# Transformer layer with perturbed experts: the key change split in four parts, the second expert's weights perturbed during the first expert's last batch, the signals' credits given by five engines

## The chip, the cores and the metric

One NeuronCore of a Trainium2 chip runs the whole program. The metric is the device time in microseconds (us), the median of several executions. The engines are TensorE (PE; PEld is its weight load), VectorE (DVE), ScalarE (ACT), GpSimd (POOL) and SyncE (SP), which issues most of the transfers.

## What is computed

Eight batches of 512 tokens with 256 features pass through a cross-attention over 64 context rows (16 heads) and a layer of 8 experts. Expert 0 has the clean weights and experts 1 to 7 all have the same perturbed weights, so the layer needs two experts, with weights p0 and the sum of the other seven probabilities.

```python
def _perturb_attractive(w, scale=0.8, sparsity=0.1):
    a = jnp.abs(w)
    k = max(1, int(n * sparsity / 2))
    s = jnp.sort(flat)
    thr_bot, thr_top = s[k - 1], s[n - k]
    tier = jnp.where(a >= thr_top, -1.0, jnp.where(a <= thr_bot, 1.0, 0.0))
    return w + scale * w * tier
...
x = x + attention(layernorm(x), ctx)           # 16 heads, softmax over 64 keys
h = layernorm(x_in) * gamma + beta             # router
probs = softmax(h @ Wr + br)
pre = x_in @ W1s[e] + b1s[e];  y = gelu(pre) @ W2s[e] + b2s[e]
out = sum_e probs[e] * y[e]
```

## The kernel before, in words

**Order.** Every engine runs a hand-written program; semaphores join them. A prologue loads weights and runs the attention of batch 0. `pipeline` then runs `body(i)` for i = 1 to 7: the attention of batch i beside the first (clean) expert on batch i - 1. `last_expert` runs the clean expert on batch 7, and a loop runs the second (perturbed) expert on batches 0 to 7, with x and the accumulator read back from DRAM.

**Products.** Each fp32 product is made of three matmuls of a high and a low part (`three`, lines 355 to 357). In an expert a batch has eight hidden products (`hidden`, 128x512 into `ps_l`) and eight output products (`output`, into `ps_y`). ACT makes the gelu and its high part in `region_c_hi` (lines 996 and 999), and the low part in `region_c_lo` is made by POOL in the first expert (`low_part`, line 1237) and by DVE in the second (line 1800). `output` waits for the low part, and `hidden` for the high part of two steps before.

**The search.** The eight thresholds (top and bottom of W1, W2, b1, b2) are found by bisection on the bits of |w|: 15 steps on the upper halfword, then 16 on the lower (`BITS`). A step is compares on DVE (`compare`, line 1455) and ACT (line 968), counts on PE (line 732), a total (line 738) and `decide` on DVE. Four steps stand in each body. Between the two rounds, in body 3 (`TURN`), DVE builds new keys from the lower halfwords: `second_round` (lines 1507 to 1536), four tensor_scalar and four tensor_tensor on 128x2048 uint16, then small instructions, the start of the new state, and only then `normalise_output(i, 0)`, for which the attention's value product `values(i, 1)` on PE waits.

**Perturbation.** In `last_expert` DVE makes the perturbed weights (`perturb`, lines 1747 to 1760: five instructions on 128x2048 fp32 for each of W1 and W2, the same on 128x8 and 128x256 for the biases), splits them into high and low parts over the clean weights (`split`, lines 1312 and 1314), splits x of batch 0 and mixes batch 7 of the first expert (`mix`, line 1440). PE's first hidden product of the second expert waits for the low part of x.

**Start.** The semaphores are counted up without a reset, so each signal first gets one batch of credit: a block of its own, in which POOL increments all 85 signals one by one (lines 368 to 372), with a barrier of all engines behind it.

## Time and profile before

| | us |
|---|---|
| median of 3 runs | 751.48 (751.09 to 755.43) |
| the profiled execution | 758.23 |
| its span, first to last instruction | 756.4 |
| PE busy in it | 672.9 (89%) |
| DVE busy in it | 517.6 (68%) |
| ACT, POOL busy | 381.6, 272.6 |

The span is what the traces show; 1.8 us of the profiled execution's own time lie around it. The profile reads in rows: the start, the time busy, the engine, the line of the program, what is written and from what, and in brackets how long the engine sat idle before it and what released it. PE's clock in a stretch is given as a share of full speed: 1.00 is 2.4 GHz, 0.5 is 1.2 GHz.

### The profile page before, as it was taken

The numbers are of one execution on the slowest core, as the hardware profiler recorded it, in microseconds if no ns is written. First come the engines' busy times: TensorE is split into PE (matmuls) and PEld (weight loads), VectorE is DVE, ScalarE is ACT, GpSimd is POOL, SyncE is SP. The second block draws the span as 40 slices with busy tenths as digits, with TensorE's granted clock in tenths as the row PEclk, the third lists the DMA queues.
The fourth block names the chain that finished last, engine by engine and source line by source line (L and its number), as shares of the span: only waits on it lengthen the run. The fifth ranks groups of instructions, "written<-read, shape, count | busy, mean of one in ns | idle before, by whom it ended". The sixth has DMA issues, their size and how long they took to land.

```text
span 756.4 us, 15501 instructions
## 1 busy us (share of the span) xinstructions
PE 672.9 (89%) x5555; PEld 613.3 (81%) x5555; DVE 517.6 (68%) x1205; ACT 381.6 (50%) x490; POOL 272.6 (36%) x284
## 2 busy tenths in 40 slices
PE   1758869999999399999999999999929999999996
PEld 1647858899889399889889899888828888898886
DVE  2778786786798869889888777653993445443452
ACT  2445226746747255855855855645304444445442
POOL 2343461673573358367366346325700000000000
PEclk9876577998999699999999998799959999999998
DMA  4996302622722440560640550231102221122221
GB/s 148 205 197 143 55 31 83 116 51 86 136 53 79 86 84 29 142 108 30 153 93 28 129 92 29 85 112 72 41 0 84 84 83 38 58 71 83 83 56 28
DMA packets 131797, 63.62 MB, mean 84 GB/s; under 512 B 104603, under 2 KB 122021, under 8 KB 131749
## 3 DMA queue, kind: packets, MB, share of 16 engines
q1 hardware_dynamic: 121652, 60.43, 32.9%
q10 hardware_dynamic: 10096, 2.56, 1.8%
q8 instruction: 29, 0.48, 0.3%
q14 instruction: 20, 0.16, 0.1%
HBM read 35.69 MB, written 23.09 MB: 78 GB/s over the span
## 4 chain that ended last, share of the span: by engine, by line
PE 67%; DVE 18%; issue 5%; SPq 4%; DMA 2%; ACT 2%; ACTq 0%; POOL 0%; DVEq 0%; POOLq 0%
PE ps_m L654 7%; PE ps_l L355 7%; PE ps_y L355 7%; PE ps_y L356 7%; PE ps_y L357 7%; PE ps_l L357 6%; PE ps_l L356 6%; PE ps_m L732 4%; DVE ind L1455 4%; PE ps_s L622 4%; PE ps_s L642 3%; DVE region_b L1430 3%; PE ps_m L694 2%; PE ps_s L355 2%; PE ps_s L357 1%
## 5 line engine op out<-in xcount | busy, mean ns | idle before, releaser
L996 ACT ACTIVATE region_b<-ps_l,bias 128x512 f32<-128x512 f32 x128 | 88.0, 687 | 172.5 <-PE ps_l L357 170.5
L355 PE MATMUL ps_y<-w_hi,region_c_hi 128*128 128x256 f32 x512 | 149.0, 291 | 0.0
L356 PE MATMUL ps_y<-w_lo,region_c_hi 128*128 128x256 f32 x512 | 146.7, 286 | 0.0
L357 PE MATMUL ps_y<-w_hi,region_c_lo 128*128 128x256 f32 x512 | 145.9, 285 | 0.0
L355 PE MATMUL ps_l<-x2s_hi,w_hi 128*128 128x512 f32 x256 | 108.8, 425 | 15.4 <-DVE x2s_lo L1314 14.8
L1237 POOL TENSOR_TENSOR region_c_lo<-region_b,region_c_hi 128x512 fp32r<-128x512 f32 x64 | 94.5, 1482 | 66.6 <-ACT region_c_hi L999 66.6
L1800 DVE TENSOR_TENSOR region_c_lo<-region_b,region_c_hi 128x512 fp32r<-128x512 f32 x64 | 44.3, 693 | 96.5 <-ACT region_c_hi L999 96.5
L357 PE MATMUL ps_l<-x2s_hi,w_lo 128*128 128x512 f32 x256 | 103.1, 403 | 0.0
L356 PE MATMUL ps_l<-x2s_lo,w_hi 128*128 128x512 f32 x256 | 102.9, 402 | 0.0
L356 PEld LDWEIGHTS ps_y<-w_lo,region_c_hi 128*128 128x128 f32 x512 | 98.6, 193 | 2.1
L355 PEld LDWEIGHTS ps_y<-w_hi,region_c_hi 128*128 128x128 f32 x512 | 98.5, 192 | 2.0
L999 ACT ACTIVATE region_c_hi<-ps_l,bias 128x512 fp32r<-128x512 f32 x128 | 87.5, 683 | 25.2 <-PE ps_y L357 25.2
L357 PEld LDWEIGHTS ps_y<-w_hi,region_c_lo 128*128 128x128 f32 x512 | 98.6, 193 | 0.0
L1455 DVE TENSOR_SCALAR ind<-key,cand 128x2048 bf16<-128x2048 uint16 x93 | 97.7, 1089 | 0.0
L1211 POOL TENSOR_TENSOR region_a<-region_a,mx 128x1024 f32<-128x1024 f32 x32 | 62.0, 1940 | 97.5 <-DVE mx L1356 97.5
L968 ACT ACTIVATE ind<-key,cand 128x2048 bf16<-128x2048 uint16 x31 | 62.0, 1999 | 48.3 <-DVE cand L1485 46.1
L654 PE MATMUL ps_m<-vbd,region_a 128*128 128x34 f32 x512 | 69.5, 295 | 15.6 <-DVE on L1366 15.4
L654 PEld LDWEIGHTS ps_m<-vbd,region_a 128*128 128x128 f32 x512 | 67.9, 214 | 16.4 <-issue 16.2
L355 PEld LDWEIGHTS ps_l<-x2s_hi,w_hi 128*128 128x128 f32 x256 | 49.6, 194 | 28.6 <-issue 16.4
L732 PEld LDWEIGHTS ps_m<-ones_bf,ind 128*128 128x128 bf16 x1488 | 45.3, 98 | 20.8 <-issue 16.6
L732 PE MATMUL ps_m<-ones_bf,ind 128*128 128x1 bf16 x1488 | 50.0, 164 | 11.3 <-DVE ind L1455 10.4
L357 PEld LDWEIGHTS ps_l<-x2s_hi,w_lo 128*128 128x128 f32 x256 | 49.5, 193 | 11.7
(200 smaller groups left out, 1228.1 us busy)
## 6 DMA issues: line engine op xcount, KB each, us to landing
qs<-q_scr SPq DMA_DIRECT2D x16, 512.0 KB, 6.5
acc_scr<-acc SPq DMA_DIRECT2D x8, 514.0 KB, 5.0
acc<-acc_scr SPq DMA_DIRECT2D x8, 514.0 KB, 3.4
xa<-in_x SPq DMA_DIRECT2D x8, 512.0 KB, 5.6
q_scr<-qn_lo SPq DMA_DIRECT2D x16, 256.0 KB, 5.0
x<-in_x SPq DMA_DIRECT2D x32, 128.0 KB, 3.9
xt_scr<-region_b SPq DMA_DIRECT2D x8, 512.0 KB, 2.6
region_b<-x SPq DMA_DIRECT2D x8, 512.0 KB, 3.1
```

The lines of the kernel that those rows point to most:

```text
L355: eng.matmul(out_ap, a[0], b[0], start=first, stop=False)
L356: eng.matmul(out_ap, a[0], b[1], start=False, stop=False)
L357: return eng.matmul(out_ap, a[1], b[0], start=False, stop=last)
L654: mm = pe.matmul(ps_m[:, 0, n * VW:(n + 1) * VW], pT[:, j % 2, n * P:(n + 1) * P], vbd[:, n, :], start=True, stop=True)
L732: mm = pe.matmul(ps_m[:, 1, s:s + 1], ind[s][:, c * P:(c + 1) * P], ones_bf[:, 0:1], start=c == 0, stop=c == WN // P - 1)
L968: act.activation(ind[3][:], key[:, key_of[rnd][3], :], ACT.Sign, bias=cand[:, 3:4], scale=-1.0, accum_out=signs[:]).then_inc(signs_summed. ...
L996: act.activation(g[:, f % 4, :], ps_l[:, f % 2, :], ACT.Gelu_apprx_tanh, bias=bias[:, e, f:f + 1]).then_inc(s["gelu"].handle, 1)
L999: act.activation(gs[0][:, f % 4, :], ps_l[:, f % 2, :], ACT.Gelu_apprx_tanh, bias=bias[:, e, f:f + 1]).then_inc(s["g_hi"].handle, 1)
L1211: pool.tensor_tensor(m, m, mx[:, j, :].unsqueeze(2).to_broadcast([P, H, CT]), ALU.subtract).then_inc(s_shifted.handle, 1)
L1237: pool.tensor_tensor(gs[1][:, f % 4, :], g[:, f % 4, :], gs[0][:, f % 4, :].bitcast(F32), ALU.subtract).then_inc(s["g_lo"].handle, 1)
L1455: dve.tensor_scalar(ind[s][:], key[:, key_of[rnd][s], :], cand[:, s:s + 1], None, ALU.is_le).then_inc(ind_ready.handle, 1)
L1800: dve.tensor_tensor(gs[1][:, f % 4, :], g[:, f % 4, :], gs[0][:, f % 4, :].bitcast(F32), ALU.subtract).then_inc(s["g_lo"].handle, 1)
```

## The change

**Credits.** Five engines give every fifth credit each, in the same block before the same barrier.

**Key change.** `second_round` becomes four parts in DVE's body 3: `end_first_round` (the prefix), then the normalisations of value tiles 0 and 1 with the queries' low parts between them, `lower_keys(0)` (half of the large instructions), more of the body, `lower_keys(1)` behind the normalisation of tile 3, and `start_second_round` (small instructions) behind the projection's low part (`low_output`).

**Perturbation.** W1 and W2 are loaded again into the search's four mark tiles `ind` (as fp32, each weight in two halves), once the last total is known, not into `region_a`. DVE perturbs W1's first half behind the statistics of batch 7 in body 7, its second half before `mix` of batch 6, and W2, the biases and the low parts between the eight low parts of the gelu of the first expert on batch 7, which move from POOL to DVE. ACT makes the high parts of the perturbed weights (four activations of 128x1024) and the normalised x of batch 7 that POOL made. The perturbed split weights go into tiles that are free by then (`qs`, `kbd`, `xhT`, `qn`), so that the clean ones stay.

**Order of the second expert.** It begins with batch 7, whose x, x's split and accumulator are still in place, and goes on with batches 0 to 6.

```diff
     with nc.Block() as credit:
+        def give(eng, share):
+            for s in signals[share::5]:
+                eng.sem_inc(s.handle, s.per)
...
         @credit.gpsimd
         def _(pool):
-            for s in signals:
-                pool.sem_inc(s.handle, s.per)
+            give(pool, 4)
...
-                wait(sp, o_product, i)
-                sp.dma_start(wagain[:, 0].rearrange("p (c f) -> p c f", c=DC), W1.rearrange("(c p) f -> p c f", p=P)).then_inc(ld_again[0], 16)
-                sp.dma_start(wagain[:, 1].rearrange("p (c d) -> p c d", c=FC), W2.rearrange("(c p) d -> p c d", p=P)).then_inc(ld_again[1], 16)
...
+                wait(sp, total_ready, sum(BITS) - 1)
+                for h in range(2):
+                    sp.dma_start(wagain[0][h], W1[h * P:(h + 1) * P, :]).then_inc(ld_again[0], 16)
+                for h in range(2):
+                    sp.dma_start(wagain[1][h].rearrange("p (c d) -> p c d", d=D),
+                                 W2.rearrange("(c p) d -> p c d", p=P)[:, h * FC // 2:(h + 1) * FC // 2]).then_inc(ld_again[1], 16)
...
             more_gelu(5)
+            if last:
+                wait(act, ln[1]["shift"], i)
+                for t in range(NT):
+                    act.activation(xh[1][:, t, :], x2[:, t, :], ACT.Identity, bias=shiftby[1][:, t:t + 1],
+                                   scale=rstd[1][:, t:t + 1]).then_inc(ln[1]["xhat"].handle, 1)
...
                 gelu(0, B - 1, f)
+                if f == 1:
+                    act.wait_ge(pw_ready, 2)
+                    for h in range(2):
+                        act.activation(w1p[0][:, h * F:(h + 1) * F], wagain[0][h], ACT.Copy).then_inc(pw_hi, 1)
+                if f == 6:
+                    act.wait_ge(pw_ready, 4)
+                    for h in range(2):
+                        act.activation(w2p[0][h], wagain[1][h], ACT.Copy).then_inc(pw_hi, 1)
...
+        def low_gelu(e, b, f):
+            s = ex[e]
+            wait(dve, s["g_hi"], b, f + 1)
+            wait(dve, s["y_step"], b if f >= 4 else b - 1, f - 3 if f >= 4 else f + 5)
+            dve.tensor_tensor(gs[1][:, f % 4, :], g[:, f % 4, :], gs[0][:, f % 4, :].bitcast(F32), ALU.subtract).then_inc(s["g_lo"].handle, 1)
...
             if turn:
-                second_round()
+                end_first_round()
...
             cmp(0, 2)
+            if turn:
+                lower_keys(0)
             probabilities(i - 1)
+            if turn:
+                normalise_output(i, 2)
...
             normalise_output(i, 3)
+            if turn:
+                lower_keys(1)
             base(0, i - 1)
             dec(0)
             low_output(i)
+            if turn:
+                start_second_round()
             cmp(1, 0, 1, 2)
             add_residual(i)
             stats(1, i, x2)
+            if last:
+                thresholds()
+                mark_weights(0, 0)
+                perturb_weights(0, 0)
...
             low_x2(i)
+            if last:
+                mark_weights(0, 1)
+                perturb_weights(0, 1)
...
         def last_expert():
...
+            low_gelu(0, B - 1, 0)
+            mark_weights(1, 0)
+            low_gelu(0, B - 1, 1)
+            perturb_weights(1, 0)
+            low_gelu(0, B - 1, 2)
+            low_weights(0)
+            low_gelu(0, B - 1, 3)
+            mark_weights(1, 1)
+            low_gelu(0, B - 1, 4)
+            perturb_weights(1, 1)
+            low_gelu(0, B - 1, 5)
+            dve.wait_ge(pw_ready, 4)
+            perturb_hidden_bias()
+            low_gelu(0, B - 1, 6)
+            perturb_output_bias()
+            low_gelu(0, B - 1, 7)
+            low_weights(1)
             probabilities(B - 1)
             base(0, B - 1)
```

DVE in body 3, from the end of the first round. `ind<-key,prefix` and `key<-ind,key` are the key change, `rs` and `on` a tile's normalisation (for PE's next value product), `qn_lo` the queries' low part. Before:

```order
L1505 COPY prefix<-cand 128x8
L1519 TENSOR_SCALAR ind<-key,prefix 128x2048 x2
L1523 TENSOR_TENSOR key<-ind,key 128x2048
L1524 TENSOR_TENSOR key<-ind,key 128x2048
...
L1501 MEMSET half 128x1
L1361 RECIPROCAL rs<-ps_m 128x16
L1366 TENSOR_TENSOR on<-ps_m,rs 128x8x16 x2
L1336 SCALAR_TENSOR_TENSOR qn_lo<-ps_s,bq,qn_hi 128x512 x2
```

And with the change:

```order
L1553 COPY prefix<-cand 128x8
L1411 RECIPROCAL rs<-ps_m 128x16
L1416 TENSOR_TENSOR on<-ps_m,rs 128x8x16 x2
L1386 SCALAR_TENSOR_TENSOR qn_lo<-ps_s,bq,qn_hi 128x512 x2
L1411 RECIPROCAL rs<-ps_m 128x16
L1416 TENSOR_TENSOR on<-ps_m,rs 128x8x16 x2
L1568 TENSOR_SCALAR ind<-key,prefix 128x2048 x2
L1571 TENSOR_TENSOR key<-ind,key 128x2048
L1572 TENSOR_TENSOR key<-ind,key 128x2048
```

Two normalisations and the queries' low part now stand ahead of the first half of the key change.

DVE further on in body 3, around the projection. `region_d_lo` is the low part for which PE's projection waits, `region_b<-b2row` the first expert's base, `x<-ps_s,x` the residual. Before:

```order
L1366 TENSOR_TENSOR on<-ps_m,rs 128x8x16 x2
L1430 SCALAR_TENSOR_TENSOR region_b<-b2row,p,region_b 128x256 x4
L1374 TENSOR_TENSOR region_d_lo<-ps_s,region_d_hi 128x1024
L1455 TENSOR_SCALAR ind<-key,cand 128x2048 x3
L1459 TENSOR_TENSOR sind<-skey,cand 128x32
L1381 TENSOR_TENSOR x<-ps_s,x 128x512 x2
```

And with the change:

```order
L1416 TENSOR_TENSOR on<-ps_m,rs 128x8x16 x2
L1568 TENSOR_SCALAR ind<-key,prefix 128x2048 x2
L1571 TENSOR_TENSOR key<-ind,key 128x2048
L1572 TENSOR_TENSOR key<-ind,key 128x2048
L1478 SCALAR_TENSOR_TENSOR region_b<-b2row,p,region_b 128x256 x4
L1424 TENSOR_TENSOR region_d_lo<-ps_s,region_d_hi 128x1024
L1578 TENSOR_SCALAR smark<-skey,prefix 128x8
L1580 TENSOR_TENSOR skey<-smark,bias 128x8
```

The second half now stands between the last tile's normalisation and the low part for the projection, and the small instructions between that and the compares.

DVE from the mix of batch 6 (`acc<-ps_y,p,region_b`) on. Before:

```order
L1440 SCALAR_TENSOR_TENSOR acc<-ps_y,p,region_b 128x256 x4
L1505 COPY prefix<-cand 128x8
L1766 CAST thr<-prefix 128x8
L1756 TENSOR_SCALAR key<-region_a 128x2048
L1757 TENSOR_SCALAR region_a<-key,thr 128x2048
L1758 SCALAR_TENSOR_TENSOR region_a<-key,thr,region_a 128x2048
L1759 TENSOR_SCALAR region_a<-region_a 128x2048
L1760 SCALAR_TENSOR_TENSOR region_a<-region_a 128x2048
```

And with the change:

```order
L1488 SCALAR_TENSOR_TENSOR acc<-ps_y,p,region_b 128x256 x4
L1759 TENSOR_TENSOR region_c_lo<-region_b,region_c_hi 128x512
L1729 TENSOR_SCALAR key<-ind 128x1024
L1730 TENSOR_SCALAR key<-key,thr 128x1024
L1731 SCALAR_TENSOR_TENSOR key<-key,thr 128x1024
L1759 TENSOR_TENSOR region_c_lo<-region_b,region_c_hi 128x512
L1735 TENSOR_SCALAR key<-key 128x1024
L1736 SCALAR_TENSOR_TENSOR ind<-key,ind 128x1024
L1759 TENSOR_TENSOR region_c_lo<-region_b,region_c_hi 128x512
L1765 TENSOR_TENSOR kbd<-ind,qs 128x1024 x2
```

The gelu's low parts (`region_c_lo`) stand on DVE now, between pieces of the perturbation of half a weight.

## Rows read from the trace of the kernel before

**Rows 1.** Page, part 4: the chain that ended last, shares of the span by engine.

```profile
PE 67%; DVE 18%; issue 5%; SPq 4%; DMA 2%; ACT 2%; ACTq 0%; POOL 0%; DVEq 0%; POOLq 0%
```

**Rows 2.** PE's waits: line, releaser: us in total, times, longest.

```profile
PE ps_m L654 <- DVE on L1366: 15.4, 2, 11.8
PE ps_l L355 <- DVE x2s_lo L1314: 14.8, 1, 14.8
```

**Rows 3.** The credit block's instructions (line 368): duration ns, start us.

```profile
L368 DVEq DRAIN  x1: 10/10/10, 0.8 to 0.8; - x1
L368 POOLq DRAIN  x1: 41/41/41, 7.8 to 7.8; - x1
L368 PEldq EVENT_SEMAPHORE  x1: 51/51/51, 8.0 to 8.0; - x1
```

**Rows 4.** DVE in order of time in body 3: start, us, what, [idle before].

```profile
245.81 1.42 DVE L1519 TENSOR_SCALAR ind<-key,prefix 128x2048 uint16<-128x2048 uint16 x2
...
249.66 1.89 DVE L1519 TENSOR_SCALAR ind<-key,prefix 128x2048 uint16<-128x2048 uint16 x2
255.33 1.22 DVE L1527 TENSOR_SCALAR smark<-skey,prefix 128x8 uint16<-128x8 uint16 x1
258.35 0.26 DVE L1361 RECIPROCAL rs<-ps_m 128x16 f32<-128x16 f32 x1
262.90 0.26 DVE L1361 RECIPROCAL rs<-ps_m 128x16 f32<-128x16 f32 x1 [2.46 <-PE ps_m L654]
270.00 0.26 DVE L1361 RECIPROCAL rs<-ps_m 128x16 f32<-128x16 f32 x1 [3.64 <-PE ps_m L654]
273.18 0.26 DVE L1361 RECIPROCAL rs<-ps_m 128x16 f32<-128x16 f32 x1 [2.40 <-PE ps_m L654]
277.00 1.21 DVE L1374 TENSOR_TENSOR region_d_lo<-ps_s,region_d_hi 128x1024 fp32r<-128x1024 f32 x1
281.50 1.28 DVE L1381 TENSOR_TENSOR x<-ps_s,x 128x512 f32<-128x512 f32 x2
```

**Rows 5.** Windows: PE, PEld, DVE, ACT, POOL busy, granted clock, DMA share, GB/s.

```profile
248.00:259.00 11.00, 0.00 (x0) 0.00 (x0) 10.56 (x24) 2.56 (x3) 6.72 (x4) 0.61 0.35 56
259.00:268.00 9.00, 8.73 (x38) 8.07 (x39) 4.72 (x22) 1.02 (x1) 0.00 (x0) 0.53 0.48 86
```

**Rows 6.** POOL in order of time in body 3: a low part beside the key change.

```profile
250.96 1.71 POOL L1237 TENSOR_TENSOR region_c_lo<-region_b,region_c_hi 128x512 fp32r<-128x512 f32 x1
```

**Rows 7.** DVE in order of time, from body 7's low part of x on.

```profile
520.91 1.22 DVE L1341 TENSOR_TENSOR x2s_lo<-region_b,x2s_hi 128x1024 fp32r<-128x1024 f32 x1
544.66 0.16 DVE L1756 TENSOR_SCALAR sabs<-bias 128x8 uint32<-128x8 uint32 x1
545.80 1.23 DVE L1756 TENSOR_SCALAR key<-region_a 128x2048 uint32<-128x2048 uint32 x1
554.35 0.29 DVE L1756 TENSOR_SCALAR key<-b2row 128x256 uint32<-128x256 uint32 x1
556.38 1.23 DVE L1312 CAST w_hi<-region_a 128x2048 fp32r<-128x2048 f32 x1
559.85 0.69 DVE L1312 CAST x2s_hi<-region_b 128x1024 fp32r<-128x1024 f32 x1
565.18 1.65 DVE L1440 SCALAR_TENSOR_TENSOR acc<-ps_y,p,region_b 128x256 f32<-128x256 f32 x4
566.75 0.68 DVE L1800 TENSOR_TENSOR region_c_lo<-region_b,region_c_hi 128x512 fp32r<-128x512 f32 x1
```

**Rows 8.** PE in order of time: the second expert's first matmul.

```profile
562.14 0.76 PE L355 MATMUL ps_l<-x2s_hi,w_hi 128*128 128x512 f32 x1 [14.82 <-DVE x2s_lo L1314]
```

**Rows 9.** Windows, columns as in rows 5, of the last batch of expert 0 and beyond.

```profile
523.90:547.40 23.50, 23.42 (x149) 20.77 (x147) 22.39 (x27) 10.13 (x16) 16.93 (x8) 1.00 0.20 68
562.00:568.00 6.00, 5.86 (x14) 4.63 (x15) 5.40 (x7) 1.55 (x3) 0.00 (x0) 0.51 0.06 23
585.40:608.50 23.10, 23.02 (x145) 20.41 (x145) 10.55 (x19) 10.13 (x16) 0.00 (x0) 1.00 0.24 69
```

More of the change, by code:

```diff
@@ L175, in build_program @@
     ind = [sb(f"ind{n}", [P, WN], BF16) for n in range(4)]
+    wagain = [[ind[2 * n + h][:].bitcast(F32) for h in range(2)] for n in range(2)]
+    mag, tier = (key[:, 2 * n:2 * n + 2].rearrange("p a n -> p (a n)").bitcast(F32) for n in range(2))
     sind = sb("sind", [P, 4, FC])
@@ L1288, in body @@
             rsqrt(1, i)
-            normalise(1, i, x2, 0, 1, 2, 3)
+            if not last:
+                normalise(1, i, x2, 0, 1, 2, 3)
             low(5)
@@ L1301, in last_expert @@
         def last_expert():
[L1302 to L1303 removed]
+            pass
         pipeline(pool, body, last_expert)
@@ new lines, in low_weights, with thresholds @@
+        def low_weights(n):
+            for h in range(2):
+                hi, lo = ([w[:, h * F:(h + 1) * F] for w in w1p], [w[h] for w in w2p])[n]
+                dve.wait_ge(pw_hi, 2 * n + h + 1)
+                i = dve.tensor_tensor(lo, wagain[n][h], hi.bitcast(F32), ALU.subtract)
+            i.then_inc(pw_lo, 1)
+        def thresholds():
+            wait(dve, cand_step, sum(BITS) - 1)
+            take_prefix()
+            dve.wait_ge(state_ready, NS + 13)
+            dve.tensor_copy(thr[:, :, 0], prefix[:]).then_inc(thr_ready, 1)
+            dve.wait_ge(thr_ready, 2)
```

191 lines of the change are left out of this document (100 added, 91 removed).

## The prediction

> **What bounds the kernel now.** The chain of work that ended last comes first: PE holds 67% of the span's time on it, DVE 18% [rows 1]. With 672.9 of 756.4 us busy, PE is the bound almost everywhere, so a change pays only where PE stands still or runs at its lower clock. Where that is, PE's list of waits shows: 15.4 us for a normalised value tile from DVE (one wait is 11.8) and 14.8 us for the low part of x in front of the second expert [rows 2]. The windows then show what such a hole costs beyond itself: after the first, PE's granted clock is 0.53 for 9 us, that is the 1.2 GHz level for nearly all of it [rows 5], and after the second it is 0.51 for 6 us [rows 9]. In full batches without a hole it is 1.00, and a batch of an expert takes 23.1 to 23.5 us [rows 9]. The third idle place is the start: POOL comes to the end of the credit block at 7.8 us and DVE at 0.8 us, and everything waits for the barrier at 8.0 [rows 3]. The change touches these three places.
>
> **The credits.** POOL spends 7.8 - 0.8 = 7.0 us on 85 increments, 82 ns each [rows 3]. Of the 85 each engine now gives 17: 17 x 82 ns = 1.4 us. PE may be slower: one semaphore instruction of its sequencer takes 51 ns where POOL's own are near 17 in the same view; with 51 - 17 = 34 ns more each, PE needs 17 x 116 ns = 2.0 us. The barrier waits for the slowest, so the gain is 5.0 to 5.6 us; I take 5.3. What follows it depends on nothing earlier and moves as a whole. No row shows two engines incrementing at once; if increments go one at a time, whoever gives them, the gain is 0. That is the lower bound, 5.6 the upper.
>
> **The key change.** From its first instruction to the residual, DVE needs 281.50 - 245.81 = 35.7 us. In that time it idles 2.46 + 3.64 + 2.40 = 8.5 us, each time for a value product of PE [rows 4], and PE makes these late since it stood still for 11.8 us and then ran at 1.2 GHz. So DVE waits for a PE that has waited for DVE. The change takes the normalisation of tile 0 from 258.35 to about 245.8: behind the prefix, whose product is ready. PE goes on at once at full clock. The work of DVE is the same: 35.7 - 8.5 = 27.2 us. To it I add what is left of idle time, about 1 us (for the high part of the queries and for value product 1, both a few tenths late), and contention: the first half of the large instructions took 249.66 - 245.81 = 3.85 us with POOL mostly idle, the second 255.33 - 249.66 = 5.7 us while POOL made low parts [rows 4, 6]. Both halves now lie beside POOL's work, which adds 5.7 - 3.85 = 1.8 us. That makes 30.0 us and a gain of 5.7 at the residual.
>
> PE gets a new hole. Its program from value product 1 to the projection is three value products, two transposes, three hidden products, one more transpose and two output products, some 15 us; with its small waits it stands before the projection at about 263. There it needs the low part `region_d_lo`, which DVE makes behind `lower_keys(1)`: 259.4 + 5.7 + 3.1 for the base (273.88 to 277.00 in rows 4, whose third wait ends at 273.18 with 0.7 of normalisation behind it) + 1.2 = 269.4. So PE idles some 6 us there and its clock may fall as in [rows 5]; the projection would take 5 us and not 3. This is mostly covered: the next thing for which PE waits, the residual, comes from DVE at 245.8 + 30.0 = 275.8, later than PE needs it. I take the gain as 6.0: 5.7, and 0.3 of the small instructions of which one took 1.22 us beside POOL at 255.33 and its fellows 0.2. Bounds: 3 (more contention, clock low to the end of the stage) and 8.5 (all idle time gone, no more contention).
>
> At this place a rule speaks against the change. The rows show that contention lengthened four large instructions by 1.8 us in all [rows 4, 6]. The Trainium skill (SBUF, "Who interferes with whom") says that DVE in a two-port mode, or with two SBUF inputs against a reading GpSimd, and GpSimd exclude each other for whole instructions. By that rule each of the four instructions could wait out one POOL low part.
>
> **The perturbation.** Now DVE needs from the mix of batch 6 until 562 for what PE waits for. The new chain of DVE starts at the low part of x, 520.91 + 1.22 = 522.1 [rows 7]. Prices: one whole weight takes 554.35 - 545.80 = 8.55 us in five instructions. A whole cast takes 1.23 and a half one 0.69 [rows 7], so the fixed part of an instruction is 2 x 0.69 - 1.23 = 0.15 us; half a weight is (8.55 + 5 x 0.15) / 2 = 4.65, say 4.8 with the semaphores between. The whole cast and subtraction take 559.85 - 556.38 = 3.47 us, so a subtraction in two halves, with the cast gone to ACT, is 2.4. Output bias: 556.38 - 554.35 = 2.0. Hidden bias: 545.80 - 544.66 = 1.1. A low part of the gelu: 0.63 in a row (0.68 by itself). Mix: 1.6. POOL has nothing left to do there, so no contention is added.
>
> W1's first half, 4.8 us, goes into DVE's idle time behind the statistics of batch 7 (it waits for the router until 520) and costs nothing; without that cover it would cost 4.8. W1's second half ends at 522.1 + 4.8 = 526.9, mix at 528.5. Then 8 low parts 5.0, two halves of W2 9.6, W1's low part 2.4, biases 1.1 + 2.0: 20.1 us, until 548.6. The last output product (12 matmuls, 1.4 us) waits for this: PE ends the first expert at 550.1 instead of 547.3. That is 2.8 us late, since between these points PE has 23.4 us of work from 523.9 [rows 9] and DVE has 26.5 from 522.1: DVE is the bound there by a little, with the PE's waits spread over the last three output products. ACT's four new activations (1.03 each by a 128x1024 activation elsewhere in the trace) delay gelu 2 and 7 by some 2 us each, while PE has output products in hand.
>
> PE then starts the second expert at 550.2 in place of 562.14 [rows 8]: 11.9 us. Its x is in place, its W1 is ready since about 537. Behind it DVE still has W2's low part 2.4, probabilities and base 2.5, mix 1.6, until 555.2; PE's first output product of the second expert waits for that mix but comes after four hidden products, 550.2 + 5.9 = 556.1. And the clock stays: before, 14 matmuls took 5.86 us at the lower level, which at 2.4 GHz would be half, 2.9 us; since PE then waits for the gelus a little, I count 2.4. Sum 14.3. Bounds: 11 (clock fell anyway or each half a fifth dearer) and 16 (no lateness of DVE).
>
> The moves of xhat to ACT, of the reload to the four `ind` tiles and of batch 7 to the front of the second expert cost nothing: four activations against four POOL instructions of the same length; W1 has from the last total near 497 until 511, where before 2 MB had from 499 until 526; and the loads of the other batches run a batch ahead as before. If W1 came late, DVE's idle time until 520 covers 4 us of it.
>
> **Sum.** 5.3 + 6.0 + 14.3 = 25.6 us. Against the profiled execution 758.23 - 25.6 = 732.6. The median of the runs is 6.75 us lower than that execution, and I take the same difference from it: 751.48 - 25.6 = 725.9, or 3.4% less.
>
> **The rivals.**
> (a) The credits bring nothing, because increments are taken one at a time. For it: no row shows them side by side. Against it: each engine's instructions in the block are its own. 751.48 - 20.3 = 731.2.
> (b) The hole in body 3 only moves to the projection. By the exclusive turns each of four DVE instructions waits for a POOL low part of 1.71 us [rows 6]: 4 x 1.71 = 6.8 us where I count 1.8 in the second half, so 5 us of my 6 are lost, and PE runs the projection and the next products at 1.2 GHz. Against it: the measured second half, beside two POOL low parts and two bias additions, was only 1.8 longer. 751.48 - 20.6 = 730.9. This is the outcome of the rule of the SBUF page named above.
> (c) The last batch of the first expert becomes bound by DVE more than counted, its instructions a fifth dearer: 26.5 x 0.2 = 5.3 us. PE's stall is spread in pieces at each output product. 731.2.
> (d) Slower than before: the waits for DVE spread through that last batch lower PE's clock and it does not come back in the second expert's loop. A batch of 23.1 us takes then 46. The gain of 25.6 is eaten after 25.6 / 23.1 = 1.1 batches at 1.2 GHz; with two such batches the time would be 751.48 - 25.6 + 46.2 = 772. For it: PE at 1.2 GHz after each hole. Against it: it came back within 6 to 9 us of steady work each time [rows 5, 9].
>
> **How the numbers follow.** My forecast, all three places within 4 us of the sum: 0.70. (a) 0.06, (b) 0.10, (c) 0.09, (d) 0.02, and 0.03 for a gain of under 7.5 us from something not seen. The range takes the three middle rivals in and goes down to all upper bounds but 1 us each: 725.9 - 5 = 721, up to 733, two of them half come true. A measurement of this kernel can tell about 1%, 7.5 us, from no change. (a), (b) and (c) are all faster by over 1%; so faster 0.95, same 0.03, slower 0.02.
>
> **What would show it.** DVE's first instruction near 2.5 us in place of 8.2. PE's wait of 11.8 us for DVE's `on` gone, and in its place one of 4 to 7 us for `region_d_lo` in body 3; DVE's half changes at 3.9 to 5.7 us each. The wait of 14.8 us gone, waits of 1 to 3 us in all for `region_c_lo` in the last batch, the first expert's end some 3 us later after the last low part of x, the second expert's first four hidden products at clock 1.00. I would be wrong if DVE's instructions beside POOL took much over 2 us, if PE's clock were under 0.9 over the last 200 us, or if W1's reload ended DVE's wait.

## The result, and the profile after

The changed kernel takes 727.1 us (median of 4 runs, 724.2 to 731.6) beside 753.1 (751.1 to 755.4) for the kernel before: a ratio of 0.966, 95% interval 0.960 to 0.972. Measured again later beside other kernels it took 725.1 us (6 runs), ratio 0.964 (0.958 to 0.970). Forecast were 725.9 us, range 721 to 733. In some executions of a kernel the mean clock is lower and the time over 1.5% longer; ratios and intervals leave these out, medians do not.

The whole program first. This is the page of the kernel after: its span, the busy times, PE's granted clock in 40 slices (tenths of full speed), and the chain that ended last.

```profile
span 724.9 us, 15487 instructions
PE 664.5 (92%) x5555; PEld 605.1 (83%) x5555; DVE 512.1 (71%) x1221; ACT 386.9 (53%) x498; POOL 257.5 (36%) x271
PEclk9776577999999979999999999989999999999999
PE 65%; DVE 19%; issue 5%; SPq 4%; DMA 3%; ACT 1%; ACTq 0%; DVEq 0%; POOL 0%; POOLq 0%
```

The chain hardly differs from [rows 1]: PE 65% where it had 67. PE has the same 5555 matmuls and is busy 8.4 us less, mostly since more of them ran at the full clock. The span is 31.5 us shorter. The profiled execution of before took 758.2 us, 5.1 above its median, so the two traces differ by 5.5 us more than the medians, which differ by 26.0.

The three places, in order of time. First the start: the increments (line 374) by engine, with duration in ns and the first and last start, then the transfer of x that follows the barrier, of after and of before (ACT, not shown, lies between SP and POOL).

```profile
L374 SPq EVENT_SEMAPHORE  x18: 17/17/17, 0.7 to 1.7; - x18
L374 POOLq EVENT_SEMAPHORE  x17: 17/17/17, 0.7 to 1.9; - x17
L374 DVEq EVENT_SEMAPHORE  x17: 21/21/21, 0.8 to 2.2; - x17
L374 PEldq EVENT_SEMAPHORE  x17: 51/51/51, 0.8 to 3.3; - x17
```
```profile
3.66 0.45 SPq L425 DMA_DIRECT2D xa<-in_x  x1
```
```profile
8.09 0.46 SPq L403 DMA_DIRECT2D xa<-in_x  x1
```

Four engines are done by 2.2 us, PE at 3.3: (3.3 - 0.8) / 16 = 0.16 us from one to the next, against 0.06 to 0.09 on the others. The barrier that ended behind 7.8 us in [rows 3] now ends at 3.6. The transfer was issued at 8.09 before: 4.4 us gained.

Next DVE in body 3, which answers [rows 4]. The large instructions of `lower_keys` are lines 1568 to 1572; line 1478 is the base, line 1424 the low part for the projection, line 1431 the residual. First the prefix before, which [rows 4] leave out:

```profile
245.60 0.17 DVE L1505 COPY prefix<-cand 128x8 f32<-128x8 f32 x1
```

And after:

```profile
240.19 0.17 DVE L1553 COPY prefix<-cand 128x8 f32<-128x8 f32 x1
240.39 0.26 DVE L1411 RECIPROCAL rs<-ps_m 128x16 f32<-128x16 f32 x1
...
244.50 2.66 DVE L1568 TENSOR_SCALAR ind<-key,prefix 128x2048 uint16<-128x2048 uint16 x2
247.20 1.63 DVE L1571 TENSOR_TENSOR key<-ind,key 128x2048 uint16<-128x2048 uint16 x1
248.75 2.30 DVE L1572 TENSOR_TENSOR key<-ind,key 128x2048 uint16<-128x2048 uint16 x1
...
256.83 0.26 DVE L1411 RECIPROCAL rs<-ps_m 128x16 f32<-128x16 f32 x1 [1.78 <-PE ps_m L683]
...
257.52 1.89 DVE L1568 TENSOR_SCALAR ind<-key,prefix 128x2048 uint16<-128x2048 uint16 x2
...
262.14 2.82 DVE L1478 SCALAR_TENSOR_TENSOR region_b<-b2row,p,region_b 128x256 f32<-128x256 f32 x4
264.88 1.21 DVE L1424 TENSOR_TENSOR region_d_lo<-ps_s,region_d_hi 128x1024 fp32r<-128x1024 f32 x1
...
270.12 1.46 DVE L1431 TENSOR_TENSOR x<-ps_s,x 128x512 f32<-128x512 f32 x2
```

The first value tile is normalised right behind the prefix. From the prefix to the residual DVE takes 270.12 - 240.19 = 29.9 us. Before it was 35.9, from the copy of the prefix at 245.60 to 281.50 in [rows 4]: 6.0 gained. PE's side, a line of its list of waits and two of its rows in order of time; the third row is that of value product 3 in a second profile of the same changed kernel:

```profile
PE ps_m L683 <- DVE on L1416: 6.4, 2, 3.7
```
```profile
253.19 3.60 PE L683 MATMUL ps_m<-vbd,region_a 128*128 128x34 f32 x16 [2.73 <-DVE on L1416]
...
266.24 0.38 PE L357 MATMUL ps_s<-wqp_hi,region_d_hi 128*128 128x256 f32 x1 [2.90 <-DVE region_d_lo L1424]
```
```profile
249.65 1.95 PE L683 MATMUL ps_m<-vbd,region_a 128*128 128x34 f32 x16 [2.73 <-DVE on L1416]
```

The wait of 11.8 us in [rows 2] is gone. In its place body 3 has 2.73 us for value tile 2, which stands behind `lower_keys(0)`, and 2.90 us in front of the projection. Behind the first of these waits PE ran at the lower clock level, 1.2 GHz: value product 3 takes 3.60 us, from 253 to 257 us the clock is 0.50, and from 253.19 to 263.35 us the granted clock is 0.68. In the second profile the wait is the same 2.73 us, but the clock is 1.00 until 251.00, falls only about 2 us after the product's start (0.57 from 251.50 to 255.50), and the product takes 1.95. The wait of 3.7 lies at 72 us, in batch 0; before, it was the other of the two in [rows 2].

Last, the second expert: PE's first matmul of it, the low part of x ahead of it on DVE, and PE's waits for the gelu's low parts.

```profile
507.01 1.22 DVE L1391 TENSOR_TENSOR x2s_lo<-region_b,x2s_hi 128x1024 fp32r<-128x1024 f32 x1
...
535.47 0.39 PE L357 MATMUL ps_l<-x2s_hi,qs 128*128 128x512 f32 x1
```
```profile
PE ps_y L357 <- DVE region_c_lo L1759: 1.4, 2, 0.8
```

From DVE's low part of x to the second expert it is 535.47 - 507.01 = 28.5 us; before, 562.14 - 520.91 = 41.2 [rows 7, 8]: 12.8 gained. The wait of 14.8 us is now two waits of together 1.4 us inside the last batch of the first expert. From there to the end of the span it is 724.9 - 535.47 = 189.4 against 756.4 - 562.14 = 194.3: 4.8 more. The windows say where the first part of that lies (PE, PEld, DVE, ACT, POOL busy, granted clock, DMA share, GB/s). Of before, the first 8 us of the second expert, then of after some of the same work:

```profile
562.00:566.00 4.00, 3.85 (x9) 3.11 (x10) 3.97 (x5) 0.84 (x2) 0.00 (x0) 0.50 0.01 2
566.00:570.00 4.00, 4.00 (x14) 2.94 (x14) 2.12 (x5) 2.42 (x5) 0.00 (x0) 0.77 0.33 132
```
```profile
542.00:546.00 4.00, 4.00 (x29) 3.66 (x29) 1.32 (x3) 2.17 (x4) 0.00 (x0) 1.00 0.00 0
```

A clock of 0.50 and 0.77 over 4 us each is 2.0 + 0.9 = 2.9 us of PE's time at full clock. After, the clock is 1.00. The other 1.9 us are shorter batches, which were no part of the change's plan. The times at which the accumulator's load is issued give a batch's length, of before (first two lines, five batches apart) and of after:

```profile
594.72 0.35 SPq L564 DMA_DIRECT2D acc<-acc_scr  x1
...
710.44 0.35 SPq L564 DMA_DIRECT2D acc<-acc_scr  x1
```
```profile
587.77 0.35 SPq L592 DMA_DIRECT2D acc<-acc_scr  x1
...
702.34 0.35 SPq L592 DMA_DIRECT2D acc<-acc_scr  x1
```

That is 115.72 / 5 = 23.14 us and 114.57 / 5 = 22.91, so 8 batches give 1.8.

The account of the two traces: start 4.4, body 3 6.0, to the second expert 12.8, behind it 4.8, together 28.0 of 31.5. The other 3.5 lie between these places: 1.0 between the first transfer and the prefix, where the code is the same, and 2.5 between the residual and x of the last batch, where it is the same but for body 7. The last section shows that stretches with the same code differ by such amounts from one execution to the next.

### The profile page after: what moved, and what is told of

Same layout as the page of the kernel before. It is cut to its first block, busy times and chain, and to the rows that moved or that the text cites. A ratio compares the mean times of both kernels' runs of the same rounds, so it can differ in the third digit from the quotient of the medians.

```text
span 724.9 us, 15487 instructions
## 1 busy us (share of the span) xinstructions
PE 664.5 (92%) x5555; PEld 605.1 (83%) x5555; DVE 512.1 (71%) x1221; ACT 386.9 (53%) x498; POOL 257.5 (36%) x271
## 4 chain that ended last, share of the span: by engine, by line
PE 65%; DVE 19%; issue 5%; SPq 4%; DMA 3%; ACT 1%; ACTq 0%; DVEq 0%; POOL 0%; POOLq 0%
PE ps_l L357 8%; PE ps_m L683 7%; PE ps_l L359 7%; PE ps_l L358 7%; PE ps_y L357 5%; PE ps_y L358 5%; PE ps_y L359 5%; PE ps_m L769 4%; PE ps_s L651 4%; PE ps_s L671 3%; DVE ind L1503 3%; DVE region_b L1478 2%; PE ps_s L357 2%; PE ps_m L723 2%; PE ps_s L359 2%
## 5 line engine op out<-in xcount | busy, mean ns | idle before, releaser
L357 PE MATMUL ps_y<-w_hi,region_c_hi 128*128 128x256 f32 x256 | 76.3, 298 | 1.4 <-DVE region_c_lo L1759 1.4
L359 PE MATMUL ps_y<-w_hi,region_c_lo 128*128 128x256 f32 x256 | 73.3, 286 | 0.0
L358 PE MATMUL ps_y<-w_lo,region_c_hi 128*128 128x256 f32 x256 | 73.3, 286 | 0.0
L769 PEld LDWEIGHTS ps_m<-ones_bf,ind 128*128 128x128 bf16 x1488 | 45.2, 98 | 19.9 <-issue 17.6
L357 PE MATMUL ps_l<-x2s_hi,w_hi 128*128 128x512 f32 x128 | 55.6, 434 | 0.1
L357 PE MATMUL ps_l<-x2s_hi,qs 128*128 128x512 f32 x128 | 52.0, 407 | 2.2 <-DVE x2s_lo L1364 1.9
L359 PE MATMUL ps_l<-x2s_hi,w_lo 128*128 128x512 f32 x128 | 51.7, 404 | 0.0
L358 PE MATMUL ps_l<-x2s_lo,w_hi 128*128 128x512 f32 x128 | 51.6, 403 | 0.0
L651 PE MATMUL ps_s<-kbd,qs 128*128 128x256 f32 x256 | 49.2, 327 | 2.2 <-DVE region_a L1400 1.2
L359 PE MATMUL ps_l<-x2s_hi,kbd 128*128 128x512 f32 x128 | 50.4, 394 | 0.0
L358 PE MATMUL ps_l<-x2s_lo,qs 128*128 128x512 f32 x128 | 50.4, 394 | 0.0
```

The source lines that it names most:

```text
L357: eng.matmul(out_ap, a[0], b[0], start=first, stop=False)
L358: eng.matmul(out_ap, a[0], b[1], start=False, stop=False)
L359: return eng.matmul(out_ap, a[1], b[0], start=False, stop=last)
L651: mm = pe.matmul(ps_s[:, m, (g % 2) * D:(g % 2) * D + D], qs[:, g, j * P:(j + 1) * P], kbd[:, n, g].rearrange("p h k -> p (h k)"), start=n ...
L769: mm = pe.matmul(ps_m[:, 1, s:s + 1], ind[s][:, c * P:(c + 1) * P], ones_bf[:, 0:1], start=c == 0, stop=c == WN // P - 1)
```

## The experiments

**Each part alone.** Three kernels each have one of the three parts on top of the kernel before. The edits are the three pieces of the diff shown above.

> The kernel before with only the credits given by five engines. Theory (the three parts of the change add up, and the start moves as a whole): the first transfer starts at 3.7 us as in the changed kernel, where it started at 8.09 [rows 3 show the barrier at 8.0], and the time falls by 4.4 us, not the 5.3 of the forecast, since PE is the last to finish its share. Rival 1 (increments are taken one at a time): first transfer at 8 us, gain 0. Rival 2 (the earlier start runs into a transfer that lands at the same time as before): first transfer at 3.7, but the first projection of body 1 at 150.9 as before, gain under 1 us.

Measured: 748.8 us against 753.8, ratio 0.994 (0.991 to 0.997), so 4.6 us (2.1 to 7.1). The transfer of x is issued at 3.66 us, as in the changed kernel, and the first projection of body 1 starts at 146.18 us, where it was 150.95: the whole gain arrives there. The increments of several engines do run side by side.

> The kernel before with only the key change split in four. Theory: body 3's residual comes 6.0 us after where it did, counted from the prefix instruction (30.0 in place of 35.9 us from prefix to residual), and the time falls by 6 us. Rival 1 (the hole moves to the projection and its cost with it): a wait of PE of 5 us or more for the low part in front of body 3's projection, PE's clock under 0.7 for the 9 us behind it, gain 3 or less. Rival 2 (what is gained in body 3 is given back in bodies 4 and 5, where DVE is late): the same 30.0 us in body 3, but under 4 us in the whole.

Measured: 746.6 us, ratio 0.990 (0.985 to 0.994), so 7.9 us, with an interval of 4.2 to 11.5. The execution that was profiled took 757.9 us, 11 more than the median, so only its order and its local waits are read: from the prefix at 244.67 to the residual at 273.19 it is 28.5 us, 7.4 less than before, and PE's wait in front of the projection 2.6. The hole does not just move.

> The changed kernel with the credits and the key change as before, so that only the perturbation, the weights' reload, and the order of the second expert's batches are changed. Theory (the term of the forecast, 14.3, and the sum of parts): gain 14.3 to 16.5 us, the upper value if the second expert's batches are each 0.25 us shorter as in the changed kernel (22.92 against 23.17 between starts of batches). Rival 1 (the clock at the second expert's start is worth nothing by itself): 12. Rival 2 (the shorter batches come from the earlier key change or credits): batches of 23.17 us here.

Measured: 736.2 us, ratio 0.976 (0.972 to 0.981), so 17.9 us (14.6 to 21.3). From the low part of x at 516.51 to the second expert's first matmul at 544.97 it is 28.5 us, as in the changed kernel, and a batch takes 22.92. Body 3 is that of before (a wait of 11.7 us for the normalised tile).

The gain is above the 14.3 to 16.5 expected. The three ratios multiplied give 0.960, the whole change 0.966 and 0.964, each with about 0.006 to either side. Within these intervals the parts add up; that one gives back 3 or 4 us of another they don't exclude, but no trace shows it. What the new order of the batches, the reload and ACT's copies bring or cost each was not measured apart.

**The credits without PE.** In the changed kernel:

```diff
-            for s in signals[share::5]:
+            for s in signals[share::4]:
...
-        @credit.tensor
-        def _(pe):
-            give(pe, 1)
```

> The changed kernel with the credits given by four engines, all but PE. In the changed kernel PE's 17 increments took from 0.8 to 3.3 us, those of SP, ACT and POOL until 1.9 at the latest, DVE's until 2.2. Theory (the barrier waits for PE, whose increments take 0.15 us each, others 0.06 to 0.08): with 21 or 22 each, DVE ends near 2.6 and the first transfer starts at 2.9 to 3.1 us in place of 3.66; gain against the changed kernel 0.6 to 0.8 us. Rival (increments slow each other, and fewer givers do not help): first transfer at 3.6 or later.

Measured: 722.9 us, ratio 0.960 (0.956 to 0.965). The slowest engine, DVE, gives its last increment at 2.6 us, and x is asked for 0.70 us earlier, by SP's row of that transfer:

```profile
2.96 0.45 SPq L421 DMA_DIRECT2D xa<-in_x  x1
```

The difference of 4.3 us to the first measurement of the changed kernel was more than the start can bring, so both were run again side by side.

> The changed kernel as it is, again, beside the next one, so that the two are measured on the same chip in the same rounds. Theory (PE's increments of 0.15 us each end the credit block 0.7 us later than four engines would): this kernel 0.5 to 1.5 us slower than the next one. Rival (the earlier difference of 4.3 us between separate calls was real, since PE's increments cost something beyond the start): 3 to 5 us slower. 725 to 728 expected.

> The changed kernel with the credits given by SP, ACT, POOL and DVE alone, again. Theory: 0.5 to 1.5 us faster than the changed kernel, the later start being all. Rival: 3 to 5 us faster, about 722 to 723, as it was measured in another call.

Measured: 725.1 and 723.9 us (0.964 and 0.960; both intervals reach 0.005 to 0.006 to either side). The difference is 1.2 us, and the first transfer again stands at 3.66 and 2.96. What the trace shows of it is 0.7 us. The 4.3 us between separate calls were for the most part scatter. Leaving PE out is right by the trace; whether it makes the whole faster is within the intervals.

**Is DVE or the hole the bound in body 3?** The second half of the keys is put behind the projection's low part, so that PE does not wait for the projection:

```diff
             normalise_output(i, 3)
-            if turn:
-                lower_keys(1)
             base(0, i - 1)
             dec(0)
             low_output(i)
             if turn:
+                lower_keys(1)
                 start_second_round()
```

> The changed kernel with the second half of the key change behind the projection's low part instead of in front of it. Theory (DVE's list is the bound of body 3 up to the residual, so the hole of 2.9 us in front of the projection costs nothing by itself): PE's wait for the low part disappears, PE waits at the compares or the residual instead, prefix to residual stays 29 to 31 us, and the time is that of the changed kernel within 1 us. Rival (the hole in front of the projection costs its length, and the clock behind it): the time falls by 2.5 to 4 us against the changed kernel, 723 to 724.

Measured: 727.6 us, ratio 0.966 (0.961 to 0.971), the same as the changed kernel. A line of PE's list of waits in this kernel, and a row of PE in order of time:

```profile
PE ps_s L357 <- DVE region_d_lo L1424: 4.1, 6, 0.8
```
```profile
268.62 0.56 PE L769 MATMUL ps_m<-ones_bf,ind 128*128 128x1 bf16 x16 [4.48 <-DVE ind L1503]
```

The wait for the projection is gone, and PE waits 4.48 us for the next marks of the search instead. From prefix to residual it is 269.81 - 239.50 = 30.3 us, not less than the 29.9 and 29.0 of the changed kernel's two profiles. So the hole in front of the projection costs nothing by itself: DVE's list of work sets the length of this stretch.

**The cover of W1's first half.** `thresholds`, `mark_weights(0, 0)` and `perturb_weights(0, 0)` go from behind the statistics of batch 7 to behind the low part of x:

```diff
             stats(1, i, x2)
-            if last:
-                thresholds()
-                mark_weights(0, 0)
-                perturb_weights(0, 0)
...
             low_x2(i)
             if last:
+                thresholds()
+                mark_weights(0, 0)
+                perturb_weights(0, 0)
                 mark_weights(0, 1)
```

> The changed kernel with the perturbation of W1's first half moved from behind the statistics of batch 7, where DVE waits for the router anyway, to directly behind the low part of x, ahead of the second half. Theory (the forecast's price for a lost cover: half a weight is 4.8 us of DVE, and DVE is the bound of the last batch of the first expert): the mix of batch 6 and all low parts are 4.7 us later, the second expert's first matmul comes 4.7 us later against the low part of x than in the changed kernel, and the time rises by 4.5 to 5 against it. Rival 1 (PE is the bound there, DVE has slack): under 2 us. Rival 2 (the waits let PE's clock fall as well): 7 or more.

Measured: 731.6 us, ratio 0.975 (0.968 to 0.982), 4.0 us above the kernel just shown, which was measured beside it; the intervals of the two ratios overlap, so the trace decides. Its low part of x stands at 504.00, and these are two rows of PE in order of time:

```profile
517.34 0.55 PE L357 MATMUL ps_y<-w_hi,region_c_hi 128*128 128x256 f32 x1 [3.98 <-DVE region_c_lo L1759]
...
537.58 0.39 PE L357 MATMUL ps_l<-x2s_hi,qs 128*128 128x512 f32 x1
```

That is 33.6 us from low part to first matmul, 5.1 more than 28.5. The cover was worth 4.8 by the forecast, and with it gone all of it shows, since DVE is the bound in that batch. PE's clock fell behind the wait of 3.98 us (0.64 from 517.30 to 521.30), but that cost nothing more, since PE had DVE to wait for again.

**The last low parts back on POOL.** DVE is relieved of its eight low parts in `last_expert` (the first of the eight lines is shown), POOL makes them as before the change.

```diff
         def last_expert():
-            pass
+            for f in range(FC):
+                low_part(0, B - 1, f)
...
-            low_gelu(0, B - 1, 0)
```

> The changed kernel with the eight low parts of the gelu of the last batch of the first expert back on POOL, the perturbation alone on DVE. Theory (contention costs what it did in the kernel before, where one weight took 12.2 us beside POOL and 8.55 alone): DVE loses 5.0 us of low parts and gains 40% on its two halves of W2 and on W1's low part, 12 x 0.4 = 4.8, and POOL's low parts take up to 2.2 us in place of 1.3: the second expert's first matmul within 1.5 us of the changed kernel's, the time within 1.5. Rival 1 (contention is small): the second expert starts 2.5 us sooner, the bound being PE. Rival 2 (exclusive turns: each POOL low part waits out a DVE instruction of up to 2.3 us and then PE waits for it): 4 us or more later.

Measured: 736.4 us, ratio 0.976 (0.971 to 0.982), 8.7 us above the kernel with the late keys of the same call; a time within 1.5 us of the changed kernel's was expected. DVE in order of time in this kernel, with a part of W2's perturbation (lines 1730 to 1737) and W1's low part (line 1766); then ACT and POOL near the end of the batch; from PE's list of waits the one for POOL:

```profile
528.23 2.19 DVE L1737 SCALAR_TENSOR_TENSOR ind<-key,ind 128x1024 f32<-128x1024 f32 x1
530.35 4.55 DVE L1766 TENSOR_TENSOR kbd<-ind,qs 128x1024 fp32r<-128x1024 f32 x2
...
540.72 1.06 ACT L1207 ACTIVATE xhT_hi<-ind 128x1024 fp32r<-128x1024 f32 x1 [6.10 <-DVE ind L1737]
...
543.96 2.02 POOL L1287 TENSOR_TENSOR region_c_lo<-region_b,region_c_hi 128x512 fp32r<-128x512 f32 x1 [7.92 <-ACT region_c_hi L1036]
```
```profile
PE ps_y L357 <- POOL region_c_lo L1287: 5.6, 1, 5.6
```

The same instructions take 1.23 and 2.35 us in the changed kernel, where POOL stands still. And ACT sits 6.1 us idle: it waits for DVE's W2 before it copies the high part, and behind that copy on ACT stands the gelu of step 7, for which POOL and PE wait. PE's first matmul of the second expert comes 548.76 - 515.32 = 33.4 us behind the low part of x, and from there to the end it is 739.3 - 548.76 = 190.5 us against 189.4: by the traces 6.0 us more than in the changed kernel. Two causes are tangled here: the queue on ACT, and DVE beside POOL. The next kernel parts them.

**The same, with ACT's copy behind the gelu.**

```diff
                 gelu(0, B - 1, f)
...
-                if f == 6:
+                if f == 7:
                     act.wait_ge(pw_ready, 4)
```

> As x8_pool (low parts of the last batch by POOL), but ACT copies the high parts of W2 behind the gelu of step 7, not before it. Theory (the 5 us that x8_pool lost come from that gelu waiting behind copies that wait for DVE, whose W2 halves take 6 to 8 us beside POOL): the PE wait of 5.6 us for the last low part goes, the second expert's first matmul comes 27 to 29 us behind the low part of x in place of 33.4, but its first output product then waits 1 to 4 us for W2's low part from a DVE that is as late as before; 731 to 734 us. Rival (POOL itself is too slow with low parts of 1.3 to 2 us): the first matmul stays over 31 us behind the low part of x, 735 to 738 us.

Measured: 730.3 us, ratio 0.967 (0.961 to 0.974), beside 725.1 for the changed kernel in the same call. The two intervals overlap; the traces show a difference of 3.9 us. PE's wait of 5.6 us is gone. The first matmul comes 537.15 - 510.72 = 26.4 us behind the low part of x, 2 us sooner than in the changed kernel. But from there to the end it is 732.5 - 537.15 = 195.4 us against 189.4. PE in order of time with its waits in brackets, and two windows of 4 us (columns as above):

```profile
541.71 0.50 PE L357 MATMUL ps_l<-x2s_hi,qs 128*128 128x512 f32 x1 [1.61 <-ACT region_c_hi L1036]
...
547.31 0.55 PE L357 MATMUL ps_y<-xhT_hi,region_c_hi 128*128 128x256 f32 x1 [2.53 <-DVE region_c_lo L1760]
```
```profile
545.00:549.00 4.00, 1.69 (x8) 1.72 (x9) 3.97 (x8) 1.16 (x2) 0.00 (x0) 0.76 0.00 0
549.00:553.00 4.00, 4.00 (x24) 3.69 (x24) 0.00 (x0) 1.17 (x2) 0.00 (x0) 0.81 0.00 0
```

PE now waits inside the second expert, for ACT's gelu (which waits for the bias from DVE) and for DVE's low part, and its clock falls. The waits are 1.61 + 2.53 = 4.1 us; the clock, 0.50 from 547.30 to 550.00 us and 0.74 for 1 us more, costs 1.6, together 5.7 of the 6 us. DVE's list from the low part of x to the end of W2's low part takes 542.39 - 510.72 = 31.7 us, with eight low parts fewer, against 536.16 - 507.01 = 29.2 in the changed kernel. The eight low parts cost DVE 8 x 0.61 = 4.9 us; POOL's presence costs it 2.5 + 4.9 = 7.4, or 0.9 for each low part. So giving them to DVE is right: it makes DVE's list shorter, not longer.

How POOL costs DVE so much, rows of the two engines show, here merged in order of time:

```profile
530.10 1.36 POOL L1287 TENSOR_TENSOR region_c_lo<-region_b,region_c_hi 128x512 fp32r<-128x512 f32 x1 [0.87 <-ACT region_c_hi L1036]
530.23 1.78 DVE L1730 TENSOR_SCALAR key<-ind 128x1024 uint32<-128x1024 uint32 x1
...
532.83 1.28 DVE L1732 SCALAR_TENSOR_TENSOR key<-key,thr 128x1024 f32<-128x1024 f32 x1
532.94 2.32 POOL L1287 TENSOR_TENSOR region_c_lo<-region_b,region_c_hi 128x512 fp32r<-128x512 f32 x1 [1.49 <-ACT region_c_hi L1036]
534.15 1.66 DVE L1736 TENSOR_SCALAR key<-key 128x1024 f32<-128x1024 f32 x1
```

Alone the two tensor_scalar take 0.69 us, the instruction of 532.83 takes 1.28, and POOL's low part 1.27. DVE's 1.78 us are the 1.23 until POOL ends at 531.46, and 0.55 of its own. POOL's 2.32 are the 1.17 until DVE ends at 534.11, and 1.15. DVE's 1.66 are the 1.11 until POOL ends at 535.26, and 0.55. The two engines take whole turns, and the one that starts second waits for the rest of the other's instruction. All seven DVE and seven POOL instructions that are delayed between 518 and 536 us in this kernel fit that within 0.1 us.

**Where W2 lies.** Why are the second expert's batches 0.23 us shorter? Their output products read the weights from `xhT` and `qn` where before they read `w`. The groups of such matmuls by form in the second expert, of before and of after (the last two numbers ahead of the idle time are the us busy and the mean ns of one):

```profile
L356 PE MATMUL ps_y<-w_lo,region_c_hi 128*128 128x256 f32 x224 | 63.7, 284 | 0.0
```
```profile
L358 PE MATMUL ps_y<-qn_lo,region_c_hi 128*128 128x256 f32 x112 | 30.9, 276 | 0.0
```

In this experiment the two pairs of tiles are declared in each other's place, so that they change addresses:

```diff
-    w2s = [sb(f"w2_{n}", [P, FC * D], F32R) for n in ("hi", "lo")]
+    xhT = [sb(f"xhT_{n}", [P, DC, S], F32R) for n in ("hi", "lo")]
+    qn = [sb(f"qn_{n}", [P, DC, S], F32R) for n in ("hi", "lo")]
```

> The changed kernel with the tiles of the first expert's W2 (w2 high and low) and those of the normalised x and the queries (xhT, qn), in which the second expert's W2 lies, declared in each other's place, so that their addresses change; instructions and order are the same. In the changed kernel an output matmul takes 277 ns in the second expert and 284 in the first, and starts follow at 0.115 and 0.120 us; the kernel before has 283 in both. Theory P (the address of the moving operand makes the difference): the second expert's outputs go to about 0.120 us and its batches to 23.3 us, the first expert's outputs to 0.115. Rival Q (it is the second expert's place in the program, or a tile of half the size): 0.115 in the second and 0.120 in the first, as before the swap. By P the time changes by under 2 us in the whole, since both experts have the same number of products.

Measured: 729.3 us, ratio 0.970 (0.964 to 0.977), and the second expert's output matmuls now take

```profile
L358 PE MATMUL ps_y<-qn_lo,region_c_hi 128*128 128x256 f32 x112 | 31.6, 282 | 0.0
```

with 23.12 us a batch. So the place of the tile matters, not its name or what was written into it. But the first expert's output matmuls, now from the place that was quick, take 280 ns where the changed kernel has 282: no mirror image. Which property of the place does it (its distance to the other tiles that are read or written at that time, say) stays open. It is worth 6 ns in 282, and 1.8 us in all.

## Why the prediction was right

The forecast was a sum of 25.6 us; the measured differences are 26.0 and 27.8 between the medians, and the median of 727.1 or 725.1 us lies at the 725.9 predicted. The three mechanisms are those predicted. The sizes are off in both directions (the parts by the traces add up to 28.0):

**Credits: 5.3 forecast, 4.4 in the trace, 4.6 timed.** The step that failed is the price of PE's increment. I added the difference of two durations (51 - 17 = 34 ns) to POOL's pace and got 17 x 116 ns = 2.0 us. Measured are 0.16 us from one to the next, so 2.6 us. The pace of an engine's increments is not their duration plus a constant: POOL has 0.075 at 17 ns, DVE 0.09 at 21, PE 0.16 at 51. PE is the last at the barrier, 1.1 us behind DVE; with four engines DVE is the last, 0.4 us later than here, and the start is 0.7 earlier. Rival (a), increments taken one at a time, is out.

**Key change: 6.0 forecast, 6.0 in the trace, 7.9 (4.2 to 11.5) timed.** The total is right, and partly by errors that cancel. The large instructions take 6.48 us in the first half and 4.62 in the second, 11.1 in all; I had 9.55 + 1.8 = 11.4. The four additions of the base, the small instructions and the compares behind the projection's low part take 2.7 + 2.0 + 2.1 us, where before, and in my sum, they took 3.1 + 3.0 + 3.4: POOL stands still from 265.8 us on. Against that DVE's idle time in the stretch is 2.9 us in place of 1, of which 1.78 is at value product 3. The step that fails here is "PE goes on at once at full clock". It does until value tile 2, which comes late behind `lower_keys(0)`. PE waits 2.73 us for it, and its clock is 0.68 over the next 10.16 us, which costs 0.32 x 10.16 = 3.3 us; then DVE waits for PE. My text let PE stand before the projection "with its small waits"; this one was not small. It is also why the hole there is 2.9 us and not 6: PE came to the projection at 266.24 - 2.90 = 263.34, where by the forecast, moved by the 5.4 us that the prefix stands earlier, it would be 257.6, and the wait and the clock explain that difference. The hole in front of the projection did not move the end, as the late second half showed. The low clock at value product 3 did: in the second profile of the same kernel the clock falls behind the same wait too, but about 2 us later and for a shorter time (0.83 over the 10.15 us from 249.65 on). There DVE does not wait for value product 3, and from prefix to residual it is 265.58 - 236.63 = 29.0 us, 1.0 less. Why the clock fell earlier in one execution than in the other stays open. The clock over 259 to 268 us is 0.88 where it was 0.53 in [rows 5].

Rival (b), the hole moving by 5 us more to the projection, is out. The rule from which it was worked out, in the page "SBUF" (section "Who interferes with whom") of the Trainium skill, is not out with it: the trace agrees with it. The rows of POOL and DVE above fit whole turns, and so do those of body 3, where DVE's 2.30 us at 248.75 are the 1.22 until POOL's low part ends at 249.97, and 1.08 of its own (1.21 alone). What was wrong is the price of a turn. I took 1.71 us, a low part that had itself waited for DVE and takes 1.27 alone, and let each of four instructions meet a whole one. An instruction of DVE loses only what is left of POOL's when it starts: in body 3 the eight large ones lost 3.4 us together, 11.1 against 2 x 3.85.

**Perturbation: 14.3 forecast, 12.8 + 4.8 = 17.6 in the traces, 17.9 (14.6 to 21.3) timed.** This is the mis-sized term, by 3.3 us, in the good direction. The start of the second expert was forecast 29.3 us behind the low part of x (520.91 to 550.2) and came after 28.5: DVE's chain until the last low part of the gelu took 533.89 - 508.15 = 25.7 us where I had 26.5. The missing clock was forecast as 2.4 and is 2.9. What I did not have at all is 1.8 us of shorter batches. The cover for W1's first half was priced at 4.8 and measured by its removal as 5.1. Rival (c), dearer instructions in the last batch, is out: without POOL beside it DVE kept its prices (0.69, 0.75, 1.28, 0.69, 1.23). With the low parts left on POOL the price would have been near right: 6.0 or 3.9 us more by the traces.

Rival (d), a clock that stays low, is out: in the window from 520.4 to 540.0 us of the changed kernel the granted clock is 1.00 in spite of the two waits, and it is 1.00 from 525.0 to the end.

The nearness of the total was luck in part: the second expert's surplus of 3.3 us stands against 0.9 missing at the start, and the parts by the traces are 2.4 more than the forecast, the first medians only 0.4. The forecast took the difference to the median from a profiled execution 6.75 us above it. Executions of the kernel before have since spread from 748 to 764 us; the medians of three calls are 753.8, 758.1 and 752.9. A forecast to 1 us says more than this kernel can be measured to. The lower end of the range, 721, takes the three upper bounds in full (5.6 + 8.5 + 16 = 30.1), and not 1 us short of each, as I wrote.

## What to carry to other kernels

When two engines wait for each other, look for the engine whose list of work fills the stretch: only shortening or moving that list pays, and a hole of the other one may be shifted, as long as its work and its clock still come back before the first engine needs them. Moving work onto the busier engine can make its list shorter, if the engine that gave it up then stops disturbing it. Before a wait is put into an engine's queue, ask what stands behind it: the gelu behind ACT's wait for W2 cost 5.6 us of PE, and moving that wait by one step removed them.

## What the runs showed of the hardware

**Semaphore increments.** Each sequencer has its own pace: 0.06 to 0.09 us on SP, POOL, ACT and DVE, 0.16 on PE, and they run side by side.

**DVE and POOL take turns.** A DVE TENSOR_TENSOR on 128x2048 uint16 takes 1.21 us alone and 1.63 to 2.30 beside POOL; a half low part of weights takes 1.22 alone and up to 2.32 beside it. Where the rows overlap, each delay is what was left of the other engine's instruction, within 0.1 us. Over the last batch of the first expert POOL's eight low parts, of 1.27 us each alone, cost DVE 7.4 us, while DVE makes the eight in 4.9.

**The place of an operand.** Output matmuls of 128x256 take 276 to 278 ns or 281 to 284 ns on average, depending on where the weights lie.

**The clock dips where PE does not wait, too.** Behind the same wait of 2.73 us in body 3 it was 0.50 at once and for 6 us in one profile of the changed kernel; in the other it fell about 2 us later, for under 4 us. Stretches with the same code differ from one execution to the next. These are two windows of 16 us at the same place of body 4, the first of the changed kernel in its second profile (spanning 332 to 348 us), the second of the kernel with low parts on POOL, which differs only from body 7 on:

```profile
332.00:348.00 16.00, 15.95 (x188) 15.23 (x187) 14.38 (x31) 12.55 (x15) 7.53 (x6) 1.00 0.09 34
```
```profile
340.00:356.00 16.00, 15.98 (x143) 15.68 (x143) 10.97 (x26) 10.00 (x11) 7.43 (x6) 0.79 0.09 34
```

PE is busy throughout in both, and the granted clock is 1.00 in one and 0.79 in the other: 0.21 x 16 = 3.4 us. PE's last wait before them was 14 us earlier or more in both, 0.8 us long. From body 4's low part for the projection to body 5's it is 55.0 to 58.0 us over all traces, 55.3 in the first of these and 58.0 in the second. What sets such a dip off in one execution and not in the next, the records do not show. It makes the spread of 7 to 19 us between runs of one kernel plausible, but that was not tested.
